# Attention's normalization: who takes the reciprocals of the softmax sums, and in how many instructions VectorE multiplies

## The reference

```
scores = einsum('bhqd,bhkd->bhqk', q, k) / sqrt(HEAD_DIM) + bias
attn   = softmax(scores)
out    = einsum('bhqk,bhkd->bhqd', attn, v)
```

## Time and profile before

| | us |
|---|---|
| median of 3 runs | 2796.4 |
| lowest and highest | 2796.13, 2797.32 |
| the profiled execution's own time | 2794.24 |
| its span, first to last instruction | 2792.4 |

### The profile page before, as it was taken

One profiled execution on the slowest core, in us unless ns is written; L12 is line 12 of the kernel. 1 busy time (PEld: TensorE's weight loads), 2 busy tenths in 40 slices (PEclk: granted clock), 3 DMA queues, 4 the chain that ended last, 5 costly groups with the idle time before them and its releaser, 6 DMA issues.

```text
span 2792.4 us, 53679 instructions
## 1 busy us (share of the span) xinstructions
PE 2683.2 (96%) x19682; PEld 1468.2 (53%) x19682; DVE 2141.0 (77%) x4443; ACT 1741.2 (62%) x3671; POOL 1255.0 (45%) x1764
## 2 busy tenths in 40 slices
PE   7989999999999999999999999999999999999998
PEld 5733376433764338643486334854358533575334
DVE  6679756997669966699667995679956799468993
ACT  4438854588545884458744687537864478643885
POOL 3415544355433554335543455434553355533453
PEclk9979999999999999999999999999999999999999
DMA  7160001600015000250003400033000330013200
GB/s 195 31 136 2 24 9 39 144 17 24 9 49 134 17 31 2 61 122 17 32 1 77 105 17 32 1 93 89 17 32 23 92 69 17 31 31 99 54 2 16
DMA packets 71429, 139.18 MB, mean 50 GB/s; under 512 B 12784, under 2 KB 49696, under 8 KB 70016
## 3 DMA queue, kind: packets, MB, share of 16 engines
q1 hardware_dynamic: 69152, 135.29, 19.4%
q10 hardware_dynamic: 2016, 0.45, 0.1%
HBM read 86.02 MB, written 38.82 MB: 45 GB/s over the span
## 4 chain that ended last, share of the span: by engine, by line
PE 70%; DVE 16%; POOL 4%; issue 4%; ACT 2%; SPq 2%; DMA 2%; POOLq 0%; DVEq 0%; ACTq 0%
PE psum L882 18%; PE psum L941 16%; DVE mx L1821 8%; PE psum L655 7%; PE psum L1008 3%; PE psum L659 3%; PE psum L916 3%; PE psum L1064 2%; PE psum L977 2%; PE psum L715 2%; PE psum L842 2%; DVE nrm L1637 2%; POOL X L1938 1%; PE psum L1049 1%; DMA SQ<-mrow 1%
## 5 line engine op out<-in xcount | busy, mean ns | idle before, releaser
L1821 DVE TENSOR_REDUCE mx<-psum 128x1 f32<-128x512 f32 x2048 | 1264.9, 684 | 60.3 <-PE psum L882 59.6
L1470 ACT ACTIVATE Z<-psum 128x512 f32<-128x512 f32 x2048 | 1109.5, 598 | 277.1 <-PE psum L916 249.2
L2030 POOL TENSOR_TENSOR Z<-Z,W_low 128x256 f32<-128x256 f32 (+1 forms) x1152 | 713.3, 642 | 665.7 <-ACT Z L1470 658.5
L882 PE MATMUL psum<-SK,SQ 63*128 63x512 f32 x2048 | 760.5, 473 | 31.1 <-DVE mx L1821 26.2
L916 PE MATMUL psum<-SQ,SK 64*128 64x512 f32 x2048 | 755.9, 469 | 11.4 <-DMA SQ<-mrow 10.9
L941 PE MATMUL psum<-Z,Vx 128*17 128x256 f32 x8192 | 641.8, 388 | 0.4 <-POOL Z L2030 0.4
L882 PEld LDWEIGHTS psum<-SK,SQ 63*128 63x128 f32 x2048 | 309.2, 189 | 479.2 <-DVE mx L1821 362.1
L916 PEld LDWEIGHTS psum<-SQ,SK 64*128 64x128 f32 x2048 | 309.4, 188 | 84.0 <-ACT Z L1470 37.1
L941 PEld LDWEIGHTS psum<-Z,Vx 128*17 128x17 f32 x8192 | 138.2, 95 | 334.1 <-issue 274.3
L1938 POOL TENSOR_TENSOR X<-X,mixed 128x512 f32<-128x512 f32 x64 | 80.5, 1268 | 249.5 <-DVE mixed L1658 249.5
L1975 POOL TENSOR_TENSOR Z<-Z 128x512 f32<-128x512 f32 x64 | 82.0, 1281 | 243.1 <-DVE Z L1692 243.1
(11 more groups left out here) (135 smaller groups left out, 3517.1 us busy)
## 6 DMA issues: line engine op xcount, KB each, us to landing
W_low<-bias_rows SPq DMA_DIRECT2D x8, 2048.0 KB, 8.7
parts<-Z SPq DMA_DIRECT2D x32, 512.0 KB
W_low<-low_parts SPq DMA_DIRECT2D x7, 1536.0 KB, 6.7
X<-L_attn_a_x SPq DMA_DIRECT2D x8, 1024.0 KB, 5.5
SQ<-parts SPq DMA_DIRECT2D x32, 256.0 KB, 7.9
SK<-parts SPq DMA_DIRECT2D x32, 256.0 KB, 10.6
SQ<-parts SPq DMA_DIRECT2D x16, 512.0 KB, 6.5
SK<-parts SPq DMA_DIRECT2D x16, 512.0 KB, 14.3
```

What stands on the lines that cost most here:

```text
L882: pe.matmul(row_bank(c), SQ[rows_of(h, MAX_ROW), h // 2, i * P:i * P + P], SK[rows_of(h, MAX_ROW), h // 2, 512 * k:512 * k + 512], start=T ...
L1470: nc.scalar.activation(ring[:, n % RING, :], col_bank(n), ACT.Exp)\
L1821: nc.vector.tensor_reduce(mx2[:, blk % 2, col, k:k + 1], row_bank(c), AX_X, ALU.max)\
L2030: nc.gpsimd.tensor_tensor(ring[:, n % RING, a:z], ring[:, n % RING, a:z], band_exp[:, 4 * hg + cols_of(s)[i], at:at + z - a], ALU.mult)\
```

## The change

What it does:

- **Blocks 0 to 5.** ScalarE copies the 16 softmax sums from PSUM into `orc`, after the second exponential of step 8k + 11 (`sums_copy`). GpSimd raises `orc` to the power -1 in place, at the head of its step 8k + 11 (`reciprocals`), with exponents from a new tile `minus_one`. VectorE waits for GpSimd, where it took the reciprocals itself.
- **Blocks 6 and 7.** VectorE still takes the reciprocals.
- **All blocks.** VectorE multiplies all four tiles with one instruction of 256 elements, where it had four of 64.
- Three semaphores replace one; one small `memset` is added at the start, and the waits for `s_zero` count six.

The diff:

```diff
+        minus_one = sb("minus_one", [P, 4, 4])
...
-        o_rc = tally("dve", "o_rc", 8)
+        o_rc = tally("pool", "o_rc", 6)
+        o_rc_late = tally("dve", "o_rc_late", 2)
+        o_sum = tally("act", "o_sum", 6)
...
+                def sums_copy(k):
+
+                    need(act, o_tp, b, k + 1)
+                    need(act, o_n, b, k)
+                    nc.scalar.copy(orc[:, :, :], sum_bank(k).rearrange("p (t h d) -> p t h d", t=4, h=4)[:, :, :, HD])\
+                        .then_inc(o_sum.sem, 1)
...
                         if i == 1 and s % 8 == 2 and s > 2 and s // 8 - 1 != 6:
                             output_copy(s // 8 - 1)
+                        if i == 1 and output_before(s) is not None and output_before(s) < 6:
+                            sums_copy(output_before(s))
...
-            for dst, value in ((power[:, :], -0.5), (nT[:, :, 0:1], 0.0),
+            for dst, value in ((power[:, :], -0.5), (minus_one[:, :, :], -1.0), (nT[:, :, 0:1], 0.0),
...
-                        nc.vector.reciprocal(orc[:, :, :], o[:, :, :, HD]).then_inc(o_rc.sem, 1)
-                        need(dve, o_rc, b, k + 1)
+                        if k < 6:
+                            need(dve, o_rc, b, k + 1)
+                        else:
+                            nc.vector.reciprocal(orc[:, :, :], o[:, :, :, HD]).then_inc(o_rc_late.sem, 1)
+                            need(dve, o_rc_late, b, k - 5)
                         dst = aO[:, 4 * half:4 * half + 4, 64 * hg:64 * hg + 64].rearrange("p t (h d) -> p t h d", h=4)
-                        for i in range(4):
-                            ins_ = nc.vector.tensor_tensor(dst[:, i], o[:, i, :, 0:HD],
-                                                           orc[:, i, :].unsqueeze(2).to_broadcast([P, 4, HD]), ALU.mult)
-                        ins_.then_inc(o_n.sem, 1)
+                        nc.vector.tensor_tensor(dst, o[:, :, :, 0:HD], orc[:, :, :].unsqueeze(3).to_broadcast([P, 4, 4, HD]),
+                                                ALU.mult).then_inc(o_n.sem, 1)
...
+                def reciprocals(k):
+
+                    need(pool, o_sum, b, k + 1)
+                    nc.gpsimd.tensor_tensor(orc[:, :, :], orc[:, :, :], minus_one[:, :, :], ALU.pow).then_inc(o_rc.sem, 1)
+
                 for s in range(NS):
+                    if output_before(s) is not None and output_before(s) < 6:
+                        reciprocals(output_before(s))
```

More of the change, by code:

```diff
@@ L609, in _ @@
             pe.wait_ge(s_first, 16 * N_FIRST)
-            pe.wait_ge(s_zero, 5)
+            pe.wait_ge(s_zero, 6)
             def raw_transposes():
@@ L1555, in constants @@
             def constants():
-                dve.wait_ge(s_zero, 5)
+                dve.wait_ge(s_zero, 6)
                 dve.wait_ge(s_const, 16 * N_CONST)
@@ L1913, in _ @@
             prime(pool, "pool")
-            pool.wait_ge(s_zero, 5)
+            pool.wait_ge(s_zero, 6)
             def rsqrts(b, n):
```

## The result

| | before | after |
|---|---|---|
| median of the runs | 2796.82 us (5 runs, 2796.13 to 2798.44) | 2932.54 us (5 runs, 2927.27 to 2934.11) |
| ratio | | 1.048, 95% interval 1.0466 to 1.0493 |
| the profiled execution's own time | 2794.2 us | 2932.76 us |
| its span | 2792.4 us | 2931.0 us |
| mean granted clock of TensorE | 0.984 | 0.956 |

The changed kernel is slower by 135.7 us. The new lines move the code: what was L882 (row products) is L885 after, L916 is L919, L941 is L944, L1821 (the reductions) is L1833, L1470 (the exponentials) is L1480. The sums' copy is L1450, the power L2034, the single multiply L1886.

A forecast was written before the change was run, and what follows sets the result against it. In attention, TensorE and VectorE were taken as both full, VectorE's delays passing into TensorE's order. The profiled 2794.2 us plus 69.6 for stalls and 31.2 for clock falls gave 2895.0; with 2.2 for the median, 2897, range 2850 to 2940.

The forecast's parts named there:

- The straight line: GpSimd's power, blocks 0 to 5: extrapolated from four and eight elements, 0.153 us per further element, 2.87 us for sixteen.
- The rule that spoke against the sum: GpSimd about twice as slow as VectorE: sixteen reciprocals would take about 0.5 us, giving 2773 us in all.
- ScalarE's copy: Blocks 0 to 5, after two exponentials: 0.264 us, ending at 988.96; delay costed at nothing, at most 10 us.
- The reading of the three banks: TensorE, allowed three row products ahead, waits for VectorE's next reduction, so VectorE's delay passes one for one into the time.
- rival E: VectorE's single multiply is issued in pieces or slowly: plus 10 us, 2907 us; chance 0.03.
- GpSimd's band multiplications: Next step's work queued behind the power: moves from 990.78 to 991.90, ends 994.69, needed from 996.03; hidden.
- every second: TensorE's clock falls at 24 of the 48 places, 1.3 us each, 31 us, between bounds of 0 and 70.
- the 0.15 taken off: Clock fall's price on TensorE: 1.45 us less 0.15 for small waits that would vanish in it, 1.3 us.
- two stretches of four microseconds: TensorE before the change: clock fell after 2.97 of 4.00 us busy, held through 2.18; about 2.1 expected with the wait.
- B: The stall without the clock: 2796.4 + 69.6 = 2866 us, with 2850 to 2878; chance 0.31.
- C: GpSimd's power grows slower than its element count, say 2.0 us: 2824 us; chance 0.08.
- D: Reciprocals ready before VectorE comes, if the power takes below 0.93 us: 23.5 us gained, 2773 us; chance 0.04.

The follow-up runs named there:

- product once: Changed kernel with the fourth column product moved ahead of the waiting row product, done once, no work added; 2925.76 us, ratio 1.0459.

## Why the prediction was right, point by point

**The place and the mechanism held.** The time came at 2932.5 for a forecast of 2897, within the range of 2850 to 2940, slower by the way that was named: VectorE waits for GpSimd's power, its reductions come late, TensorE waits for them, and its clock falls in part of the places.

**GpSimd's power: right.** The straight line through the earlier trace rows gave 2.87 us; it is 2.902. Twelve and fourteen elements, with 2.27 and 2.59, lie on the same line, so the exponent of -1 costs what -0.5 does. The rule that spoke against the sum, the Trainium skill's page "GPSIMD Engine Reference", section "4.1 Engine selection", has GpSimd about twice as slow as VectorE for an elementwise add, multiply or maximum of two inputs. It doesn't carry over to this operation: 2.90 us for the power against 0.25 for VectorE's reciprocals is a factor of 12. The plain multiply of the same sixteen elements took 0.221 us, less than VectorE's reciprocals; it is the power that is dear, not the engine.

**ScalarE's copy: priced too high.** 0.178 us, where I took 0.264 from a read of other shape. Put back by the 48.83 us by which the place lies later in this trace, the power ends at 991.80 for a forecast of 991.90, though it is 0.03 us longer; VectorE's multiply then starts 0.10 us behind it and not 0.04, and the next reduction 0.03 us earlier than forecast, 1.4 us in all. (The waits view's mean of 1.84 us counts from the recorded end of the reductions. The forecast's 1.94 counts from 990.00, here 1038.83, and in that count the place has 1040.73 - 1038.83 = 1.90.) The delay in ScalarE's order cost nothing, as taken: with the multiply in the power's place a block takes 20.61 us, and that is the 20.90 of the single multiply alone less the 0.29 that VectorE's reciprocals held it.

**VectorE and TensorE: right.** The next reduction is 1.42 us late for 1.45, 48 x 1.42 = 68.2 us for 69.6, and TensorE's idle time 1.78 us for 1.9. The reading of the three banks as a pass of one for one stands: over 0.63 us less of power the block shortened by 0.62. The new multiply takes 0.34 us from start to start, 0.33 predicted; rival E, the multiply in pieces or slow, is out.

**Blocks 6 and 7, GpSimd's band multiplications, the rest:** worth nothing, as costed: with the power cheap or asked for later the kernel is faster than before, so nothing else in the change costs anything. Outside attention the profiled execution was 3.6 us longer, which the forecast had at nothing. The control "product once", with the same power, was only 0.7 us longer there, so this is not taken for an effect of the change; 6.1 us more at half clock outside attention (39.3 for 33.2) account for part of it.

**The clock: the term that was mis-sized.** The step took "every second" place, 24 x 1.3 = 31.2 us, between none and all. The price of a fall came out right, 1.30 us between a block with and one without, but partly by luck: the length was half of 6.8 us by assumption, and no row showed the 0.15 taken off. Nor do all falls before last 6.8 us: the seventh takes 10.2. The number of falls was wrong: a fall behind 43 places by the records, 49 by the time at half clock, and 66.8 us (135.0 less 68.2). That is 35.6 us more than forecast, and so in size all of the missing 35.5; the stall's 1.4 us too much, the 3.6 outside attention, and a median 0.2 us below the profiled execution where I added 2.2, cancel among themselves. I had split the difference between two stretches of four microseconds that bounded nothing: one before a fall and one that held. The doses show how coarse that was: at 1.14 us of idle time the count is 2 of 48, at 1.46 it is 33, and from 1.54 to 1.97 it is 43 to 47. With the stalls near 1.8 us, all 48 would have been the better value, 2794 + 70 + 62 = 2926, plus 2 us for the median; no row of the forecast could have told that.

**Rivals.** B had its stall right, and the run with the gap filled landed 2 us from its 2866; it fell on the clock. C, a power that grows slower, fell with the line. D, faster, was right in its condition and its size: with 0.22 us in the power's place the time is 2774.8 for 2773. It only doesn't apply to a power.

## What to carry to other kernels

Before work moves to an idle engine, set its length *there* against the slack of the engine that will ask for it, at that place: here 2.9 us against about 1 until VectorE asks, or 1.5 to come out even. Where it is longer, ask for the result later; one step's delay turned a loss of 136 us into a gain of 18. And where TensorE is full, cost a repeated stall twice, once for its own length and once for the clock it may bring down at every repetition; the count may be nearly none, two in three or nearly all, so give both ends of the range, and look for a run with stalls of that length before choosing a value between.

## What the runs showed of the hardware

- **The clock falls after idle times shorter than the fall.** With TensorE otherwise busy for over 20 of a block's 22 us and its clock at 1.00, an idle time of 1.14 us left it up (2 falls in 48), 1.46 us brought it to 0.5 behind 33 places of 48, and 1.54 to 1.97 us behind 43 to 47. In the change the fall started anywhere between 0.2 us before work resumed and 1.8 after, mostly lasted 3.4 us, and cost 1.3 us. The Trainium skill's page "TensorE: Matmul & The Clock Gate", section "A second HAM failure mode: psum-queue depth-cycling", tells of a kernel in which TensorE idles briefly but often between groups of matmuls, and whose clock swings between its two levels; the traces here agree, with 43 swings in 48 places.
- **Useless matmuls can pay.** Five products without a purpose in each gap saved 58 us.
- **A power on GpSimd costs by the element:** 1.03 us for 4 per partition, 1.65 for 8, 2.27 for 12, 2.59 for 14, 2.90 for 16, against 0.22 us for a plain multiply of 16.
- **Four small instructions against one on VectorE:** 4 x 64 elements hold it for 0.53 us, 1 x 256 for 0.34.
